# Attention and spiking MLP on one core: scores and value products both in tiles of 64 rows and 32 columns

## What is computed

```
xn = layernorm(x)
q  = per head (16 heads of 16 features): xn_h @ Wq_h.T
attn = softmax(q @ q.T / NORM)          # NORM = 0.25, so the scores are times 4; keys and values are q too
s  = concat_h(attn @ q) @ Wp.T + bp
y  = relu(xn @ W_fc.T)**2 @ W_proj.T    # 256 -> 1024 -> 256
n  = spikes of 5 integrate-and-fire steps with input y, /5
out = x + s * silu(n)
```

## Time and profile before

| | |
|---|---|
| median of 3 runs | 2662.93 us |
| the profiled execution | 2663.11 us, span 2658.1 us |
| mean granted TensorE clock | 0.988 of 2.4 GHz |
| TensorE busy | 2491.2 us (94%) |
| ScalarE busy | 2111.4 us (79%) |
| VectorE busy | 1391.3 us (52%) |
| GpSimd busy | 728.0 us (27%) |
| exps (L713) | 2048, 1985.8 us |
| value matmuls (L555) | 8192, 997.1 us |
| score matmuls (L581) | 4096, 639.7 us |

### The profile page before, as it was taken

How to read it: one execution, slowest core, us unless ns; L and a number is a source line. 1 busy time by engine, 2 the same in 40 slices (tenths; PEclk the granted TensorE clock), 3 DMA queues, 4 the chain that set the end, 5 groups by cost and what they waited for, 6 DMA issues and landing times.

```text
span 2658.1 us, 55164 instructions
## 1 busy us (share of the span) xinstructions
PE 2491.2 (94%) x18944; PEld 966.0 (36%) x18944; DVE 1391.3 (52%) x2453; ACT 2111.4 (79%) x2309; POOL 728.0 (27%) x682
## 2 busy tenths in 40 slices
PE   5999999999999999999999999999999999999997
PEld 2333333333333333333333333333333333333333
DVE  5545645456454555545455464554645645456463
ACT  3888888788887878878878887878887888788885
POOL 3313323133231332312222232331313323033240
PEclk8999999999999999999999999999999999999998
DMA  3021020211202012030110302102021020211200
GB/s 119 25 69 45 24 83 8 75 40 37 77 1 86 28 45 69 1 97 17 57 57 10 89 17 66 48 17 82 17 69 45 29 85 1 77 38 39 95 1 26
DMA packets 61079, 127.05 MB, mean 48 GB/s; under 512 B 15378, under 2 KB 16659, under 8 KB 58387
## 3 DMA queue, kind: packets, MB, share of 16 engines
q1 hardware_dynamic: 60818, 123.50, 15.0%
HBM read 89.36 MB, written 34.08 MB: 46 GB/s over the span
## 4 chain that ended last, share of the span: by engine, by line
PE 80%; issue 5%; ACT 5%; DVE 3%; ACTq 0%; DVEq 0%
PE acc L555 34%; PE aux L459 26%; PE scores L581 19%; ACT e L713 4%; PE aux L534 1%; DVE h_t L801 0%; DVE r L795 0%; DVE xn_t L782 0%; DVE q_hi L761 0%; DVE q_lo L763 0%; ACT v_stage L665 0%; PE aux L524 0%; ACT xn_t L658 0%; DVE cnt L811 0%; ACTq L292 0%
## 5 line engine op out<-in xcount | busy, mean ns | idle before, releaser
L713 ACT ACTIVATE e<-scores 128x1024 f32<-128x1024 f32 x2048 | 1985.8, 1022 | 497.2 <-PE scores L581 493.5
L555 PE MATMUL acc<-e,v_ones 128*32 128x512 f32 x8192 | 997.1, 605 | 0.2
L581 PE MATMUL scores<-query_stack,key_stack 49*128 49x512 f16 x4096 | 639.7, 384 | 55.0 <-issue 30.9
L1021 POOL TENSOR_TENSOR r_squared<-r 128x512 f32<-128x512 f32 x256 | 266.6, 1041 | 801.6 <-DVE r L795 788.6
L581 PEld LDWEIGHTS scores<-query_stack,key_stack 49*128 49x128 f16 x4096 | 168.8, 93 | 699.0 <-ACT e L713 544.8
L555 PEld LDWEIGHTS acc<-e,v_ones 128*32 128x32 f32 x8192 | 215.3, 109 | 481.3 <-issue 479.0
L459 PE MATMUL aux<-w_proj,h_t 128*128 128x256 f16 x3072 | 374.5, 273 | 12.6 <-ACT v_stage L665 12.6
L459 PE MATMUL aux<-xn_t,w_fc 128*128 128x512 f16 x1536 | 372.6, 382 | 2.2 <-DVE h_t L801 2.2
L459 PEld LDWEIGHTS aux<-w_proj,h_t 128*128 128x128 f16 x3072 | 283.5, 98 | 114.7 <-issue 66.0
L1024 POOL TENSOR_TENSOR h_t<-r_squared,h_t 128x512 f16<-128x512 f32 x256 | 309.0, 1207 | 36.7
L795 DVE TENSOR_SCALAR r<-aux 128x512 f32<-128x512 f32 x256 | 174.8, 683 | 241.9 <-PE aux L459 239.2
(11 more groups left out here) (66 smaller groups left out, 1152.4 us busy)
## 6 DMA issues: line engine op xcount, KB each, us to landing
key_stack<-q_scratch SPq DMA_DIRECT2D x384, 64.0 KB
query_stack<-q_scratch SPq DMA_DIRECT2D x384, 64.0 KB
x_tok<-x SPq DMA_DIRECT2D x16, 1024.0 KB, 4.9
x_out<-x SPq DMA_DIRECT2D x32, 512.0 KB, 3.8
out<-x_out SPq DMA_DIRECT2D x32, 512.0 KB, 2.6
q_scratch<-q_hi SPq DMA_DIRECT2D x32, 256.0 KB
q_scratch<-q_lo SPq DMA_DIRECT2D x32, 256.0 KB
query_stack<-c_scratch SPq DMA_DIRECT2D x128, 4.0 KB
```

Of the source, the lines that this page charges most:

```text
L555: ins = nc.tensor.matmul(acc[unit % 2][STRIP * n:STRIP * (n + 1), :], v_ones[:, j, G * g + n, :], e[:, tile, n % 2, :], start=j == 0, stop ...
L581: return nc.tensor.matmul(bank, key_stack[base:base + 49, at, j * P:(j + 1) * P], query_stack[base:base + 49, at, half * HALF:(half + 1) * ...
L713: nc.scalar.activation(e[:, tile % NE, :, :], scores[tile % 2][:, :, :], ACT.Exp, scale=4.0 if exact else SCORE_SCALE).then_inc(s.exp_done, 1)
L1021: nc.gpsimd.tensor_tensor(r_squared[:, :], tile, tile, ALU.mult).then_inc(s.rsq_set, 1)
```

## The change

Scores: each 128 key columns are cut into four strips of 32, so that a matmul takes 49 rows and 32 keys and writes one strip of 32 partitions; 16 matmuls in a step instead of 4. Values: each product is cut into rows 0 to 63 and 64 to 127 of the keys. The lower rows accumulate in `acc[0]`, the upper ones in `acc[1]`, for every unit; 8 products in a step instead of 4. VectorE copies `acc[0]` to `acc_sum`, adds `acc[1]`, and transposes `acc_sum`. A unit's first value product waits until the addition of the unit before is done. TensorE's waits in `pv` and `score_step` are set apart.

```diff
 # pv
-                        wait(pe, s.acct_set, b * 8 + (unit - 1))
+                        wait_apart(pe, s.acct_set, b * 8 + unit)
                         if half == 0:
-                            pe.wait_ge(s.vones_set, b * 4 + (g + 1))
-                    pe.wait_ge(s.exp_done, b * 128 + (2 * i + 2))
+                            wait_apart(pe, s.vones_set, b * 4 + (g + 1))
+                    wait_apart(pe, s.exp_done, b * 128 + (2 * i + 2))
                     for n in range(G):
                         tile = (2 * i + n // 2) % NE
-                        ins = nc.tensor.matmul(acc[unit % 2][STRIP * n:STRIP * (n + 1), :], v_ones[:, j, G * g + n, :],
-                                               e[:, tile, n % 2, :], start=j == 0, stop=j == TT - 1)
+                        for low, base in enumerate(BASES):
+                            ins = nc.tensor.matmul(acc[low][STRIP * n:STRIP * (n + 1), :], v_ones[base:base + 64, j, G * g + n, :],
+                                                   e[base:base + 64, tile, n % 2, :], start=j == 0, stop=j == TT - 1)
 # score_step, and the new score_strip
+                def score_strip(bank, head, half, j, c):
+                    base, at = BASES[head % 2], head // 2
+                    return nc.tensor.matmul(bank[STRIP * c:STRIP * (c + 1), :],
+                                            key_stack[base:base + 49, at, j * P + STRIP * c:j * P + STRIP * (c + 1)],
+                                            query_stack[base:base + 49, at, half * HALF:(half + 1) * HALF], start=True, stop=True)
...
-                        wait(pe, s.exp_done, b * 128 + (tile - 1))
-                        for n in range(2):
-                            ins = score(scores[tile % 2][:, n, :], G * g + 2 * pair + n, half, j)
+                        wait_apart(pe, s.exp_done, b * 128 + (tile - 1))
...
+                            for c in range(G):
+                                for n in range(2):
+                                    ins = score_strip(scores[tile % 2][:, n, :], G * g + 2 * pair + n, half, j, c)
 # normalise
-                    nc.vector.transpose(acc_t[:, :, :].rearrange("p c r -> p (c r)"), acc[unit % 2][:, :]).then_inc(s.acct_set, 1)
+                    nc.vector.tensor_scalar(acc_sum[:, :], acc[0][:, :], 1.0, None, ALU.mult).then_inc(s.part_set, 1)
+                    dve.wait_ge(s.part_set, b * 16 + (2 * unit + 1))
+                    nc.vector.tensor_tensor(acc_sum[:, :], acc[1][:, :], acc_sum[:, :], ALU.add).then_inc(s.acct_set, 1)
                     dve.wait_ge(s.acct_set, b * 8 + (unit + 1))
+                    nc.vector.transpose(acc_t[:, :, :].rearrange("p c r -> p (c r)"), acc_sum[:, :]).then_inc(s.part_set, 1)
+                    dve.wait_ge(s.part_set, b * 16 + (2 * unit + 2))
```

More of the change, by code:

```diff
@@ L161, in __init__ @@
         self.gate_set = sem(f"{way}_gate_set")
+        self.part_set = sem(f"{way}_part_set")
         self.acct_set = sem(f"{way}_acct_set")
@@ L228, in build @@
         e = sb("e", [P, NE, 2, HALF], FP32)
+        acc_sum = sb("acc_sum", [P, HALF], FP32)
         acc_t = sb("acc_t", [P, HALF // STRIP, STRIP], FP32)
@@ L579, in score @@
                     base, at = BASES[head % 2], head // 2
-                    if not exact:
-                        return nc.tensor.matmul(bank, key_stack[base:base + 49, at, j * P:(j + 1) * P],
-                                                query_stack[base:base + 49, at, half * HALF:(half + 1) * HALF], start=True, stop=True)
                     nc.tensor.matmul(bank, q_rows[j // 4][base:base + DH, at, j % 4 * P:(j % 4 + 1) * P],
@@ L593, in score_step @@
                         tile = 2 * i + pair
-                        wait(pe, s.exp_done, b * 128 + (tile - 1))
-                        for n in range(2):
-                            ins = score(scores[tile % 2][:, n, :], G * g + 2 * pair + n, half, j)
+                        wait_apart(pe, s.exp_done, b * 128 + (tile - 1))
+                        if exact:
+                            for n in range(2):
+                                ins = score(scores[tile % 2][:, n, :], G * g + 2 * pair + n, half, j)
+                        else:
+                            for c in range(G):
+                                for n in range(2):
+                                    ins = score_strip(scores[tile % 2][:, n, :], G * g + 2 * pair + n, half, j, c)
                         ins.then_inc(s.scored, 1)
```

## The result

The changed kernel takes 2972.63 us (median of 4 runs, 2969.87 to 2975.66), the kernel before 2664.82 (median of 4) in the runs beside it: a ratio of 1.116, with a 95% interval of 1.114 to 1.118. The prediction was 2933 in a range of 2785 to 3075, slower with a chance of 0.92. The sum was 38 us short of the measured loss of 308.

What follows compares the result with a forecast made beforehand. The prediction took TensorE, busy for 94% of the span, to bound the kernel. It summed 2663 + 246 (accumulators) + 14 (VectorE's added operations) + 48 (clock) - 38 (switches) = 2933 us, range 2785 to 3075.

Steps and rivals of the forecast that it cites:

- The accumulator wait: At unit ends, a unit's first value product waits for VectorE's copy and addition of the unit before: 246 us lost.
- The clock: After the three stalls over 3 us of each batch TensorE's clock falls: 48 falls at 1.0 us, 48 us lost.
- The switches: One shape removes switches between scores and values; ordinary rounds gain nothing, waiting for ScalarE: 38 us gained, at best 123.
- VectorE's added operations elsewhere: Where no stall is, they delay VectorE's later work: relu of a batch's first fc tile, 0.9 us each, 14 us lost.
- The back edge: At the loop's end, TensorE idles 2.1 to 2.7 us; no term in the sum, up to 35 us more in a rival.
- Rival 3: Accumulator wait decides, clock falls after every stall, longer loop body costs at each back edge: 3040 us, chance 0.14.
- Eight tiles stream together: Score and value steps on TensorE stay two groups of eight each, 0.22 and 0.43 us a group: cost 0.
- Rival 2: Eight tiles do not stream together on TensorE; score steps take 0.43 us more: 3270 to 3370 us, chance 0.12.
- Waits apart: Separate wait instructions on TensorE take 0.14 us against about 0.05 fused, nothing where met earlier; counted within other terms.
- Rival 1: VectorE's accumulator read is hidden, no unit stalls, and the switches pay: 2625 us, down to 2540, chance 0.08.
- the main term: TensorE idle before `acc` matmuls until VectorE's add, about 100 times, 1.6 to 4.7 us long: 246 us.

Runs made afterwards that it cites:

- e_wait: Kernel before, but a unit's first value product waits for VectorE's read of the unit just before, not the one before that: 2904.5 us, ratio 1.088.
- e_wait_ops: Kernel before with that nearer wait and VectorE's copy, addition (same bank again) and transposition in place of one transposition; old tiles: 3015.9 us, ratio 1.129.
- e_split: Changed kernel with VectorE's copy and addition put ahead of the round's other work, the transposition and the rest left behind it: 2653.7 us, ratio 0.9965.
- e_strips: Kernel before with only the scores in strips and their waits apart; values, banks and VectorE as before: 2689.1 us, ratio 1.009.
- e_apart: Kernel before with only the four waits of scores and values on instructions of their own: 2666.6 us, ratio 1.001.

## Why the prediction was right, step by step

- **The accumulator wait: right.** 246 us forecast; 254.8 measured in the changed kernel (the 29.2 us after units 3 and 0 with it), 103 times where "about 100" was forecast, by the mechanism named, with the longest stalls at units 6, 0 and 4. From the start of the read to the next value product 1.66 us against 1.6: the two operations took less (1.41, forecast 1.48) and the step from the addition's end to the matmul more (0.25, forecast 0.14). e_wait and e_wait_ops show it alone; e_split takes it away.
- **The clock: right.** 48 us forecast, 54 by the estimate above. The way there was not the forecast's: it counted 48 falls at 1.0 us, and the trace has 40 stretches at the lower level where the kernel before has 13, so 27 more at 2.0 us each.
- **The switches: the size that failed.** Forecast 38 us gained, and the balance below leaves nothing for them. Ordinary rounds were to stay as they were; they lost 0.05 us each. The second tile starts 2.65 us into the round, as the sum had it (2.64; 2.62 before); from there to the other products it is 0.34 us instead of 0.31, which the sum left at its old size. The trace shows most of that: the last of the eight strips starts 0.02 us after the first. e_strips has the same 0.03 (0.57 against 0.54). With short exps the whole 0.22 us per round is there.
- **VectorE's added operations elsewhere: mechanism right, size half.** 14 us forecast, for relus of a batch's first fc tile; the wait for h_t rose from 19.2 to 46.2 us, 27.
- **The back edge: left out of the sum, 28 us to the good.** The idle time there fell from 30.9 to 3.3 us. It hangs together with the term before: in the one batch whose first scores still idled 1.6 us, the wait for the first relu is not there; in most others it is 1.92 us. Rival 3 had the back edge cost more; it cost less.
- **Eight tiles stream together: right.** Scores 0.45 us to the values, two value steps 1.71 us. Rival 2 falls. The Trainium skill (TensorEngine Tiling (Array Packing), Feature Incompatibilities) excludes the fast weight load here. The trace shows no price for it: the score loads took 92 ns each where the whole ones took 93, neither longer nor the 27 ns that the prediction estimated for a strip, and they start so close together that eight fitted into each group.
- **Waits apart: right within what can be seen.** e_apart sees nothing within 0.3%, at a clock that varied from run to run (0.984 to 0.994).
- **Rival 1** needed the read to begin within 1.3 us of the last value product. e_split makes just that true, and its 2654 us is 29 above rival 1's 2625, since the switches' 38 us are missing there too. It had the wait right for another kernel.

So the sum of the added span, 312.6 us (2970.7 - 2658.1), is 255 for the accumulators, 27 for h_t, 54 for the clock, 28 less at the back edge, 4 less for xn_t (28.9 to 25.3), and 8 for all the rest, the switches among it. Against the forecast that is 9, 13 and 6 us more on the first three, and the 38 us of the switches that were not there; the back edge hid 28 of these 66. That the forecast was not further off is in that part luck. Only rival 3 had a term for the back edge, and that with the wrong sign.

## What to carry to other kernels

When a change takes away a second buffer, the price is not the consumer's work but where that work stands in the consumer's queue: read the start times of the old read, add the new operations, subtract the producer's next start. If the queue is written by hand, cut the consumer's work at the point where the buffer is free and move only that part ahead; here that was worth 319 us. And before crediting a gain on the busiest engine, follow one round to the next wait that ends last: 0.23 us per round was real, and all of it turned into waiting for an exp. Before crediting a small gain to the edit, compare the clocks as well: most of what the tiles seemed to gain here was time at 2.4 instead of 1.2 GHz. And where an instruction waits for several things, the releaser that the profile names can be the wrong one: 29 us of the main term stood under ScalarE's name.

## What the runs showed of the hardware that was not expected

- Eight tiles of 64 rows and 32 columns stream side by side for two different operations, and no switch shows between the two: 16 float16 matmuls of 49x32 in 0.45 us and 32 float32 ones in 1.71 us.
- Packing is as good as the order of issue: with other scores between heads 1 and 2 of a value step, half of the next tile's strips started 0.19 us late and the round took 4.89 us instead of 4.73.
- With the old tiles, idle time of TensorE cost two fifths to a half more than its length: 169 us of stalls brought 162 us more at 1.2 GHz (64 to 226), 146 of them with matmuls running, and cost 244.5 us of span.
